# Angles on VectorE with their rounding on ScalarE, weights by group, and reordered gap and late stages in a gated cross-attention and mixture-of-experts layer

## The reference

```
q = rms_norm(layernorm(x) @ Wq.T)     # 16 heads of 128
k = rms_norm([context; x] @ Wk.T)     # 4 heads of 128; layernorm(x) in the place of x
v = [context; x] @ Wv.T
q, k = rope(q, pos_x), rope(k, [pos_ctx, pos_x])    # cos and sin of pos * inv_freq, 64 frequencies
x = x + tanh(g_xattn) * softmax(q k.T / sqrt(128)) v @ Wo.T
h = layernorm(x)
p = softmax(h @ w_router); the two best of 8 experts, their shares made to sum to 1
routed = 2.5 * sum over the two of share * (silu(h @ w_gate[e]) * (h @ w_up[e])) @ w_down[e]   # width 176
shared = (silu(h @ ws_gate) * (h @ ws_up)) @ ws_down                                          # width 352
x = x + tanh(g_ffn) * (routed + shared)
```

## Time and profile before

| | |
|---|---|
| median of 3 runs | 1284.08 us |
| profiled execution: time, span | 1284.96 us, 1283.2 us |
| TensorE busy | 1210.8 us, 94% |
| VectorE busy | 1039.7 us, 81% |
| ScalarE busy | 878.6 us, 68% |
| GpSimd busy | 949.3 us, 74% |
| granted clock of TensorE, mean | 0.989 |

### The profile page before, as it was taken

The page is one execution under the profiler, slowest core; times in us unless marked ns, Lnnn a source line. Parts: engine busy times, 40 slices in busy tenths (PEclk is TensorE's granted clock), DMA queues, the critical chain, the costliest instruction groups (busy, mean ns, idle before and its releaser), DMA issues.

```text
span 1283.2 us, 31482 instructions
## 1 busy us (share of the span) xinstructions
PE 1210.8 (94%) x8825; PEld 1150.5 (90%) x8826; DVE 1039.7 (81%) x3015; ACT 878.6 (68%) x3745; POOL 949.3 (74%) x1143
## 2 busy tenths in 40 slices
PE   0399999999999999999999999999999889999998
PEld 0389999999999999999999999999999789999898
DVE  8878888888888888888888888888888477777444
ACT  3577777777777777777777777777777336666322
POOL 7577888888887888888888887888887215556554
PEclk9799999999999999999999999999999899999999
DMA  5512222223333322222323333222235826554574
GB/s 191 169 34 72 87 92 86 90 86 110 93 102 106 96 86 86 86 90 90 95 94 112 104 98 123 90 72 72 76 105 177 274 72 188 165 165 149 174 238 141
DMA packets 127093, 148.78 MB, mean 116 GB/s; under 512 B 13760, under 2 KB 107328, under 8 KB 126016
## 3 DMA queue, kind: packets, MB, share of 16 engines
q1 hardware_dynamic: 112192, 126.10, 32.4%
q0 software_dynamic: 6528, 17.90, 3.7%
q10 hardware_dynamic: 8320, 4.19, 1.1%
HBM read 67.26 MB, written 80.89 MB: 115 GB/s over the span
## 4 chain that ended last, share of the span: by engine, by line
PE 85%; DVE 9%; ACT 2%; issue 1%; DMA 1%; POOL 1%; SPq 0%; ACTq 0%; DVEq 0%; POOLq 0%
PE b_o L1651 13%; PE b_kv L1600 13%; PE b_q L1586 12%; PE b_sc L1625 8%; PE b_aT L1640 8%; PE b_pT L1633 5%; PE b_qT L1614 4%; PE b_q L1829 3%; PE b_kv L1829 3%; PE b_aT L1761 3%; PE b_q L1743 2%; PE b_kT L1610 2%; PE b_sc L1743 2%; DVE sincos L413 1%; ACT probs L939 1%
## 5 line engine op out<-in xcount | busy, mean ns | idle before, releaser
L1600 PE MATMUL b_kv<-w_group,kv_in_hi 128*128 128x256 f32 x1024 | 213.5, 306 | 9.8 <-DVE k_sin L1187 9.8
L1586 PE MATMUL b_q<-w_group,kv_in_hi 128*128 128x512 f32 x512 | 173.3, 420 | 31.9 <-DVE kv_in_lo L1173 29.3
L1600 PEld LDWEIGHTS b_kv<-w_group,kv_in_hi 128*128 128x128 f32 x1024 | 168.7, 192 | 17.4 <-DVE k_sin L1187 10.5
L722 POOL TENSOR_TENSOR qk_r<-qk_me,minus_half 128x6 f32<-128x6 f32 x128 | 174.3, 1361 | 10.0
L939 ACT ACTIVATE probs<-b_sc,neg_max 128x128 f32<-128x128 f32 x512 | 180.1, 371 | 1.5 <-DVE neg_max L1211 1.5
L726 POOL TENSOR_TENSOR q_rot<-q_rot,q_sin 128x512 f32<-128x512 f32 x128 | 164.3, 1283 | 9.7 <-DVE q_sin L1201 4.8
L1651 PE MATMUL b_o<-wo_hi,aT_hi 128*128 128x256 f32 x512 | 154.3, 301 | 0.5 <-DVE aT_lo L1225 0.2
L933 ACT ACTIVATE pT<-b_pT 128x512 f32<-128x512 f32 x128 | 76.6, 599 | 112.6 <-PE b_pT L1633 110.7
L1600 PE MATMUL b_kv<-w_group,kv_in_lo 128*128 128x256 f32 x512 | 145.0, 283 | 0.0
L1651 PE MATMUL b_o<-wo_lo,aT_hi 128*128 128x256 f32 x512 | 143.0, 279 | 0.0
L1651 PE MATMUL b_o<-wo_hi,aT_lo 128*128 128x256 f32 x512 | 143.0, 279 | 0.0
(11 more groups left out here) (252 smaller groups left out, 3966.1 us busy)
## 6 DMA issues: line engine op xcount, KB each, us to landing
xs_scratch<-zeros SPq DMA_DIRECT2D x34, 1032.0 KB, 6.3
s_in<-xs_scratch SPq DMA_DIRECT2D x72, 129.0 KB
yT_scratch<-yT SPq DMA_DIRECT2D x32, 256.0 KB, 2.0
yS<-yT_scratch SPq DMA_DIRECT2D x32, 256.0 KB, 3.6
routed<-ys_scratch SPq DMA_DIRECT2D x32, 256.0 KB, 3.6
w_hi_all<-w_scratch SPq DMA_DIRECT2D x3, 1536.0 KB, 8.7
x_in<-in_x SPq DMA_DIRECT2D x32, 128.0 KB, 2.4
ctx_raw<-in_ctxT SPq DMA_DIRECT2D x32, 128.0 KB, 2.6
```

The costliest lines, as they stand in the source:

```text
L722: nc.gpsimd.tensor_tensor(qk_r[g % 2][:], qk_me[:], minus_half[:, 0:REP + NB], ALU.pow).then_inc(r_ready, 1)
L1586: last = nc.tensor.matmul(b_q[:], kv_in[p][a][:, c, 1:3, :], wq_of(b, gg)[:, c, :], start=(c == 0 and (a, b) == PASSES[0]), stop=(c == DC ...
L1600: last = nc.tensor.matmul(b_kv[:, s * 2 * HD:(s + 1) * 2 * HD], kv_in[p][a][:, c, 2 * s:2 * s + 2, :], wkv_of(b, c)[:, g % KVH, :], start= ...
```

## The change

1. GpSimd makes no angles. VectorE makes all 8 chunks in the order 0, X0, 1, X0+1, 2, X0+2, 3, X0+3. The product (`angle_products`) is a step of its own, done ahead of the rest. For the first two chunks VectorE rounds to whole turns (`first_turns`); for the other six ScalarE does it with two Identity activations (`whole_turns`), with ROUND and -ROUND as bias from a small tile (`rounder`). ScalarE waits for each step of a chunk (`step`), now also between the absolute value and the sine.
2. The last two chunks' angles (3 and X0+3) are made inside unit 0, behind its maxima, and ScalarE's tables of them, the tanh of the gates and the change to the exponentials' table too.
3. Weights are loaded and split by group: the first group of Wq and of Wk and Wv by two loads, the rest by two more; the pieces are Wq and Wk/Wv of group 0, of group 1, and so on. Groups 2 and 3 are split in low parts inside units 0 and 1, Wo inside units 0 to 2, and TensorE waits for each piece where it needs it. The router's weights count in `ld_const`, now 12.
4. In a pair, GpSimd's waits for scatters and zero fills are moved behind its key sum, and `cos_table`, `layer_rstd2` and `sin_table` ahead of the scatter.
5. SyncE: the zero fills are moved (the spare rows' to the first pair, the last tile's to the last pair, ahead of `load_hi`); `load_hi(2)` and `load_hi(3)` stand ahead of the store of tile 30's token splits, inside the last pair.
6. Gap: ScalarE runs a silu on one number before it copies the last probabilities, which changes its table there. The table of slots comes from a mask by expert (`below_e`), one product and one sum (`upto`) in place of a copy and three shifted additions, and from `worth`, so that `s_a` and `s_b` fall away. `shared_down(6)` and `shared_hidden_T(7)` come behind the first slot's transposes, `shared_down(7)` behind the first slot's gate/up.
7. Late stage: odd tiles have b_o as output bank, and VectorE adds tile t-2 where it added t-1.

```diff
-        CHUNKS_V = (0, X0, 1, X0 + 1, 3, X0 + 3)
-        CHUNKS_P = (2, X0 + 2)
+        CHUNKS = [c for n in range(X0) for c in (n, X0 + n)]
...
+            def angle_products(*chunks):
+                for c in chunks:
+                    nc.vector.tensor_tensor(sincos[c][:, :, 1, :],
+                                            pos_f[:, c * CH:(c + 1) * CH].unsqueeze(2).to_broadcast(shape),
+                                            invf_s[:].unsqueeze(1).to_broadcast(shape), ALU.mult).then_inc(product_v, 1)
...
+            def whole_turns(c):
+                act.wait_ge(product_v, CHUNKS.index(c) + 1)
+                turn, a = sincos[c][:, :, 0, :], sincos[c][:, :, 1, :]
+                step(nc.scalar.activation(turn, a, ACT.Identity, bias=rounder[:, 0:1], scale=1 / (2 * np.pi)))
+                nc.scalar.activation(turn, turn, ACT.Identity, bias=rounder[:, 1:2]).then_inc(turns_ready, 1)
...
             split_hi(pieces[0:1])
+            context_hi(0, 0, 0)
+            split_hi(pieces[1:2])
+            normed_hi(0, 0)
             tables(0)
-            context_hi(0, 0, 0)
             tables(X0)
-            split_hi(pieces[1:3])
-            normed_hi(0, 0)
-            split_hi(pieces[3:6])
-            tables(2)
-            tables(1)
-            split_hi(pieces[6:7])
+            for c in (1, X0 + 1):
+                whole_turns(c)
+            split_hi(pieces[2:4])
+            for c in (2, X0 + 2):
+                whole_turns(c)
             query_squares(0, 0)
-            split_hi(pieces[7:8])
             key_squares(0, 0)
             values_out(0, 0)
+            tables(1)
             tables(X0 + 1)
+            split_hi(pieces[4:6])
+            query_squares(1, 1)
+            for c in (3, X0 + 3):
+                whole_turns(c)
+            tables(2)
             tables(X0 + 2)
-            split_hi(pieces[8:9])
-            query_squares(1, 1)
-            tables(3)
-            tables(X0 + 3)
+            split_hi(pieces[6:10])
...
+                    if first and u == 0:
+                        tables(3)
+                        tables(X0 + 3)
+                        exponent_table()
                     exponentials(n, g)
...
+            angle_products(0, X0)
             normalize_x(0, 0)
+            first_turns(0, X0)
             angles(0, X0)
+            angle_products(1, X0 + 1)
             split_lo(pieces[0:1])
             context_lo(0, 0)
-            angles(1, X0 + 1)
-            split_lo(pieces[1:3])
+            split_lo(pieces[1:2])
             normed_lo(0, 0)
-            split_lo(pieces[3:4])
+            angle_products(2, X0 + 2)
             dve.wait_ge(ld_const, 16 * N_CONST)
...
-            split_lo(pieces[4:6])
+            angles(1, X0 + 1)
+            split_lo(pieces[2:4])
+            angle_products(3, X0 + 3)
+            turn_queries(0, 0, 0, 0)
+            turn_keys(0, 0, 0)
+            angles(2, X0 + 2)
             layer_stats(1, 0, 1)
...
                     score_max(n, g)
+                    if first and u == 0:
+                        angles(3, X0 + 3)
+                        split_lo(pieces[4:6])
+                    if first and u == 1:
+                        split_lo(pieces[6:8])
...
                     if not (first and p == 0):
                         store_x1(t - 1, 1 - p)
+                    if last and p == 1:
+                        for g in range(2, KVH):
+                            load_hi(g)
+                    if not (first and p == 0):
                         store_yT(t - 1, 1 - p)
...
+            nc.scalar.activation(gates_raw[:, 0:1], gates[:, 0:1], ACT.Silu)
             probs_out(4 * TILES - 1, 3)
...
-            shared_down(EARLY - 1)
-            slot_T(0, 1)
+            shared_down(EARLY - 2)
+            shared_hidden_T(EARLY - 1)
...
                     slot_gate_up(m, p, expert[q])
+                    if first and q == 0:
+                        pe.wait_ge(hT_lo, EARLY)
+                        slot_T(0, 1)
+                        shared_down(EARLY - 1)
...
             for t in range(EARLY, TILES):
                 hidden(t)
-                if t > EARLY:
-                    add_shared(t - 1)
+                if t > EARLY + 1:
+                    add_shared(t - 2)
                 hidden_lo(t)
+            add_shared(TILES - 2)
             add_shared(TILES - 1)
```

More of the change, by code:

```diff
@@ L396, in w2_piece @@
             return [w[:].rearrange("p c n -> p (c n)")[:, some] for w in (raw, lo)] + [wide]
[L398 to L420, removed]
-                a = sincos[c][:, :, 1, :]
-                nce.tensor_scalar(a, a, PI_BELOW, -PI_BELOW, ALU.min, ALU.max).then_inc(done, 1)
-        CHUNKS_V = (0, X0, 1, X0 + 1, 3, X0 + 3)
-        CHUNKS_P = (2, X0 + 2)
+        CHUNKS = [c for n in range(X0) for c in (n, X0 + n)]
         @block.sync
@@ L752, in _ @@
             layer_rstd(0, 0)
-            pool.wait_ge(pos_ready, 1)
-            for c in CHUNKS_P[:2]:
-                angles(c)
             pool.wait_ge(wsin_ready, 4)
@@ L807, in pair @@
                               .then_inc(below_cut, 1)
-            walk(pool, pair)
+            walk(pool, pair, start=2)
             again = wd_lo[AGAIN:P, FC:DN, :].rearrange("p (e c) d -> p e c d", c=EFC)[:, :, 1, :]
@@ L1416, in pair @@
                     sum_inverse(n, g)
-                    if first and u == 0:
-                        split_lo(pieces[9:10])
+                    if first and u in (1, 2):
+                        split_lo(pieces[9 + u:10 + u])
                     if not (first and u == 0):
@@ L1501, in _ @@
                 hidden_lo(t - 1)
-            add_shared(EARLY - 2)
-            for p in range(2):
-                for o in (P, P + AGAIN):
-                    V.memset(s_hid[p][:, o + REST:o + AGAIN], 0.0)
-            hidden_lo(EARLY - 1)
             def slot_lo(m, p):
@@ L1540, in _ @@
             slot_dest(0, 0)
-            add_shared(EARLY - 1)
+            for p in range(2):
+                for o in (P, P + AGAIN):
+                    V.memset(s_hid[p][:, o + REST:o + AGAIN], 0.0)
+            add_shared(EARLY - 2)
+            hidden_lo(EARLY - 1)
             slot_lo(1, 1)
             slot_dest(1, 0)
+            add_shared(EARLY - 1)
             def slots(k, first, last):
@@ L1701, in pair @@
                         attend(n - 1, g - 1)
+                    if first and u < 2:
+                        pe.wait_ge(w_lo, 2 * (u + 2) + 2)
                     if not (end and g >= 2):
```

241 lines of the change are left out of this document (128 added, 113 removed).

## The result

The changed kernel takes 1303.68 us (median of 4 runs, 1303.02 to 1305.39), the kernel before beside it 1283.88 (1283.48 to 1286.13): ratio 1.0153, 95% interval 1.0135 to 1.0170. 1270.2 was forecast, 1264 to 1277 the range. It is 19.8 us slower, where 14 less were expected.

A forecast was written before the change was run, and what follows sets the result against it. Attention was taken as bound by TensorE's own work, so only late stage, gap and head could move: -4.4 - 7.7 - 1.8 = -13.9 from 1284.96 gives 1271.1; the median, 0.9 below, gives 1270.2 us; range 1264 to 1277.

The forecast's parts named there:

- Edits that cost nothing: Steady loop, zero fills and first weight loads: GpSimd's moved waits and the other reordering there add no time.
- Rival E: Steady loop: moved GpSimd waits stall TensorE on late scatters or fills; at 0.6 us a tile, 1288.8 us; chance 0.03.
- attention is bound by TensorE's own work: Attention, 160 to 500 us: TensorE busy 339.19 of 340 us, so reordering other engines can give no time there.
- The head: Start, up to steady state: angles taken off GpSimd bring the first exponentials 2.3 us earlier; -1.8 us in all.
- Identity needed no table: Head, ScalarE: a rival said Identity needs another table than Sin, +2.6 us, 1272.8 us; chance 0.03.
- Rival B: Head: constants late behind trig stores, or ScalarE's extra passes before the tables; head +2.5, 1274.5 us; chance 0.13.
- The gap: Between attention and experts: earlier weights, a shorter slot table and moved downs save 7.7 us.
- (b): Gap, table of slots: VectorE's chain, which TensorE waits for, gets shorter; -1.0 us.
- (c): Gap, down(6) and down(7): first-slot work fills the second wait for the low half and 0.2 of the first; -1.2 us.
- Rival C: Gap: part 3 of the weights lands late behind yS loads or scatters; gap -4, 1274 us; chance 0.06.
- The late stage: Its start: the later addition and second output bank remove TensorE's 2.65 us wait and 1.7 of slow clock; -4.4 us.
- The end stays: End of the late stage: the last addition waits for the last matmul as before, so no change there.

The follow-up runs named there:

- experiments 1 to 3: scatter_first, 1272.98 us; the changed kernel with only unit 1's scatter put back in front, 1275.24 us; before_scatter_last, 1308.90 us.
- before_scatter_last: The kernel before with GpSimd's scatters moved behind `sin_table` and `layer_rstd2`, all else as before: 1308.90 us, ratio 1.0195.
- scatter_first: The changed kernel with each scatter put back ahead of `layer_rstd2` and `sin_table`, its three waits ahead of the key sum: 1272.98 us, ratio 0.9915.
- (12): scatter_first with the rounding of chunks 1 to 3 on VectorE, not ScalarE: 1274.09 us, ratio 0.9916 against the kernel before.
- (10): scatter_first with the first load of wo issued behind the loads of tile 0's trig tables: 1267.37 us, ratio 0.9863 against the kernel before.
- (11): The kernel of (10) with VectorE's two splits of wo one unit later, in units 2 and 3: 1266.98 us, ratio 0.9871 against the kernel before.
- old_head: The kernel before with only the edits of the gap and the late stage: 1275.15 us, ratio 0.9929.
- (9): The kernel before with the late stage's edits alone: 1281.89 us, ratio 0.9984.
- (5): The kernel before with one always-met GpSimd wait added ahead of `cos_table` in each tile: 1284.60 us, ratio 1.0000.

## Why the prediction was wrong

**The step that failed** is "Edits that cost nothing: the moved waits of GpSimd in a pair (83% busy; the scatters that they ask for are a unit old, 2.9 us to land)". It asked whether what the waits wait for is late. It is not. It did not count that an instruction, the issue of a scatter, 1.06 to 1.20 us, had moved behind `layer_rstd2`, whose own wait for VectorE it used to fill. The steady loop was put at 0 and is +19.0. Rival E named the place ("the scatter comes behind `layer_rstd2` and `sin_table`") and the size (0.6 us a tile; 19.0 over 29.75 tiles is 0.64), but gave it landing times as its cause and 3 in 100. Shown by experiments 1 to 3. A scatter's late landing, rival E's own cause, shows only in tile 30 of before_scatter_last.

**The premise under it**, "attention is bound by TensorE's own work, and no edit to another engine's order in it can give time", was wrong in both directions. The busy share of 99.8% hid stalls: the ends of matmuls are modelled, and tiles of 29.93, 29.37 and 29.19 us show 0.15 us of idle time, none and none. Against scatter_first the changed kernel costs 28.7 us in the loop, of which the difference to the kernel before shows 19.0 only, since the kernel before had its own 9.65 to lose; after has slow products too, in 15 tiles. The slack of 1.2 us a unit was an average over four units. In unit 1 GpSimd's idle time lies in the wait for VectorE's variance, so the scatter behind it made the next scales 1.31 us later (4.28 against 2.97 behind k_rot).

**The head**, -1.8 forecast, +6.9 measured. The constants came at 23.09 (23.0), Identity needed no table, the rounding passes cost little where they are (12). Wrong was the landing of the trig stores, counted at the median of 3.4 us: the second took 11.3, behind 1 MB of wo and the constants. That is 6.05 of the 8.5 us by which scatter_first's unit 8 is late (10). Of the rest, a split of wo that VectorE and GpSimd do side by side takes 3.40 where 1.13 was counted, but moving the splits doesn't bring that back (11), so how the last 2.5 us divide stays open. Rival B, constants and stores late, had the mechanism, with +2.5 as its price. The head also differs by up to 2.9 us between kernels that have the same one: unit 1 starts at 66.33 in after and at 69.23 in scatter_first, behind a store's issue of 0.38 and 3.59 us on ScalarE (10). So part of the 6.05 is that issue, which the prediction had not counted either; why it is long in one kernel and short in the other stays open.

**The gap**, -7.7 forecast. It is -7.8 in scatter_first and -7.3 in old_head: right. In the changed kernel it is -4.9, because the late k_rot of unit 127 costs 2.02 and slow clock behind it. Of its parts, the weights no longer wait, the normalization of probs(127) is 0.56 late (0.6 forecast), and the four downs, which waited 0.77, 1.70, 1.17 and 0.96, wait 0.36, 1.23, 0.95 and not at all: 2.1 less, of which 0.2 comes back at the next transposes, for (b) and (c), forecast at 2.2. Rival C is out.

**The late stage**, -4.4 forecast, -4.75 in TensorE's part. "The end stays" failed: +1.75 by GpSimd's drain, -3.0 in all (9).

With the loop at -9.65, the head at +8.5, gap -7.8, late -4.8 and tail +1.8, scatter_first ends 2.8 us from the forecast. That is errors that cancel, and no support for the forecast's terms of head and loop.

## What to carry to other kernels

When a diff reorders an engine's queue, list for each moved instruction what idle time it used to stand in, and look for the wait that it filled: an instruction moved from before a wait to behind it costs its whole length, on an engine that looks to have slack. A TensorE that is 99.8% busy in the profile can still lose 0.6 us in 11 of 29 tiles; compare the starts of one instruction from tile to tile before calling the loop bound, and look for pairs of VectorE and GpSimd operations that start within 0.05 us of each other. Then see whether TensorE's next start slips with them: one such pair cost 0.6 us a tile, another 0.08. Take a store's landing time from what else is in flight then, not from its median.

## What the runs showed of the hardware

- Who starts first, by 0.014 us or more, decides 0.86 us: VectorE's 128x384 product takes 0.56 or 1.42, GpSimd's 1.4 or 1.02. An operation on two elements a partition is held up as well, from 0.16 to 0.55 and, in other tiles, up to 0.94.
- GpSimd's queue takes 6.74 us from its last instruction's start to its end, in every kernel here. It is hidden only where the last store comes later.
- A satisfied wait ahead of an instruction doesn't move its start when the engine is still busy (5).
- The 512 KB trig store took 11.3 us with wo's load ahead of it, 6.3 without, 3.2 as the median of all 8. Its issue held ScalarE's queue 0.38 us in some kernels and 2.5 to 3.6 in three of the four with that load ahead.
- A scatter issued at 988.45, with the DMA share at 1.02 from 994 to 1000, took 11.1 us to land; the median of all 64 in before is 2.9.
